# Moving the split of the contexts from GpSimd to VectorE, and loading the query bias in rows, in a cross-attention kernel on one Trainium2 core

## The chip, the cores and the metric

The kernel runs on 1 core of one Trainium2 chip. A time is device microseconds (us) of one execution, and a kernel's time is the median of its runs. The core has five engines that the text names: TensorE (PE in the profile; PEld are its weight loads), VectorE (DVE), ScalarE (ACT), GpSimd (POOL) and SyncE (SP), which issues most of the DMAs. An engine name with a q (SPq, ACTq) is that engine's sequencer issuing a DMA.

## The reference

The inputs are x (16, 100, 128), a context (16, 1444, 128), weights Wq, Wk, Wv (128, 1024), Wo (1024, 128), and biases. For each of 16 batches and 16 heads of 64:

```
q = (pre_q @ Wq + bq).reshape(b, ql, H, D_Q)
k = (pre_k @ Wk + bk).reshape(b, kl, H, D_Q)
v = (pre_k @ Wv + bv).reshape(b, kl, H, D_Q)
scores = jnp.einsum('bqhd,bkhd->bhqk', q, k) / jnp.sqrt(jnp.float32(D_Q))
attn = jax.nn.softmax(scores, axis=-1)
ctx = jnp.einsum('bhqk,bkhd->bqhd', attn, v).reshape(b, ql, H * D_Q)
out = ctx @ Wo + bo
x = pre_q + out
```

A layer norm over the last axis with gamma and beta follows. pre_q is x and pre_k the context.

## The kernel before

**The algebra.** Keys and values are never formed. A prologue multiplies each head's Wq and Wk parts into a 128x128 matrix a_sb, and its Wv and Wo parts into m_sb. A batch's queries are then x times a_sb plus a bias term (gb_sb, made from Wk and bq), its scores are those queries against the context itself, and its output is (attention times context) times m_sb. Operands in 32 bits are split into a high and a low half in 16 bits (c_hi and c_lo of the context, g_hi and g_lo of the queries, p_hi and p_lo of the attention), and three products of halves stand for one.

**Tiles.** The 1600 rows (16 heads by 100 queries) of a batch are cut into tiles of 128 rows. Two batches make 25 tiles, the middle one shared, so there are N = 200 tiles. The loop over n runs on all engines at once, each with its own program. For tile n TensorE makes scores (nine matmuls of 482 columns, line 631); VectorE takes the row maximum (L917); ScalarE takes the exponentials (L1072) with their sum; VectorE inverts the sum (L923, L925); ScalarE writes p_hi (L1080) and the tail of p_lo (L1087); VectorE writes the rest of p_lo (lo_part, L932). SyncE transposes p_hi and p_lo by DMA (pt_hi, L420; pt_lo, L429), in one queue in the order written: pt_lo of tile n-1, then pt_hi of tile n. Four tiles later (LAG) TensorE multiplies them with the context (L670), two tiles at a time, and ScalarE takes the result (L1110).

**What waits for what.** scores(n) writes the half of PSUM that exp(n-2) reads, so it waits for it. exp(n) waits for the row maximum, and for the p_lo of tile n-2, whose buffer it overwrites. VectorE's order in step n is: row_max(n), lo_part(n-1), row_inverse(n), then whatever that step has besides.

**Windows.** The 12 or 13 tiles of a batch are its window w; r is the place of a tile in it. Work for the next batch w+1 is spread over the window: query projections at r = 1 to 4 on TensorE, copied by ScalarE (L1096), split by GpSimd; c_hi of the next context by ScalarE in three groups of four context tiles at r = 4, 6, 7 (L1016); sums of magnitudes of the context after it by ScalarE at r = 5 and 8 (L1023); c_lo by GpSimd in two instructions for each group: c_raw times alpha into c_scaled (L1254), minus c_hi (L1258); then c_tail (L1243, L1245). SyncE transposes c_hi (ct_hi, L400) at r = 7 and c_lo (ct_lo, L411) at r = 8 (9 in the first window). The first context's c_lo is made by VectorE in the prologue, one instruction for each group (L881). TensorE has the output projection of batch w-1 at r = 6 to 9.

**The prologue.** Banks of PSUM are numbered jobs: 0 to 3 transposed weights, J_A and J_B the head products (two banks each), J_X the first x transposed, with the bias product beside it (query_bias, L543), then the query projections J_G (L480). Each is emptied by VectorE or ScalarE. bq goes by two DMAs, element by element, into bq_pairs, whose columns stand for heads (L1000). TensorE's order is J_A, query_bias, spread_context_max, the x transposes, J_B, J_G.

Of the kernel before, what the change touches and what calls it, by code (L numbers as in the profile page):

```python
# [12 lines left out]
P = 128  # L13
# [11 lines left out]
def cross_attention_kernel(nc, x, ctx_in, Wq, bq, Wk, bk, Wv, bv, Wo, bo, gamma, beta, out):  # L25
# [45 lines left out]
    CT_HI_AT = 7  # L71
    CT_LO_AT = 8
# [66 lines left out]
    with ExitStack() as es:  # L139
# [58 lines left out]
        c_scaled = sb("c_scaled", [P, TG * D])  # L198
# [5 lines left out]
        p32 = sb("p32", [P, P32S, SCOREW])  # L204
        bq_pairs = sb("bq_pairs", [P, PAIRS, 2])
# [23 lines left out]
        s_bq = sem("bq_loaded")  # L229
        s_bvl = sem("bv_loaded")  # L230
# [44 lines left out]
        s_cs = sem("context_scaled")  # L275
# [35 lines left out]
        J_A, J_X, J_B = 4, 6, 7  # L311
        J_G = J_B + 2
# [6 lines left out]
        BY_SCALAR = [1, 3, J_A, J_A + 1, J_X, J_B + 1, J_V1, J_M2]  # L319
# [142 lines left out]
        def _(pe):  # L462
# [76 lines left out]
            def query_bias(bank):  # L539

                pe.wait_ge(s_bq, 32)
                for c in range(PAIRS):
                    mm = pe.matmul(bank[:, XG * QL + 2 * c:XG * QL + 2 * c + 2], w_t[1][:, c, :], bq_pairs[:, c, :],  # L543
                                   start=True, stop=True)
                return mm
# [278 lines left out]
        def _(dve):  # L824
# [46 lines left out]

            empty(0)
# [4 lines left out]
            empty(J_B)  # L877
# [56 lines left out]

            def take_rows(b):
# [16 lines left out]
            for n in range(N + 1):  # L952
# [40 lines left out]
        def _(act):  # L993
            for half in range(2):
                cols = slice(half * D_H // 2, (half + 1) * D_H // 2)
                act.dma_start(w_raw[1][:, cols], Wk[:, cols]).then_inc(s_w[1][half], 16)
            act.wait_ge(s_bqz, 1)
            for i in range(2):
                rows = slice(HEAD_DIM * i, HEAD_DIM * i + HEAD_DIM)
                act.dma_start(bq_pairs[rows, :, i:i + 1], bq.rearrange("(c i p o) -> i p c o", i=2, p=HEAD_DIM, o=1)[i],  # L1000
                              allow_slow_non_contiguous=True).then_inc(s_bq, 16)
# [38 lines left out]
            for k in (1, 3, J_A, J_A + 1):  # L1040
                empty(k)
            a_sum(0)
            empty(J_X)
            act.activation(gb_sb[:, :], job_bank(J_X)[:, XG * QL:XG * QL + H], ACT.Copy, scale=SCALE).then_inc(s_gb, 1)
            for g in range(NT):
                context_hi(0, g)
            empty(J_B + 1)
# [127 lines left out]
        def _(pool):  # L1175
# [54 lines left out]
            def leave_m_lo(g):  # L1230
                heads, at = slice(HG * g, HG * g + HG), c_scaled[:, :].rearrange("p (n w) -> p n w", w=P)
# [15 lines left out]
            def context_lo(b):  # L1247
                par = b % 2
                pool.wait_ge(s_al, b + 1)
                for g in range(NT):  # L1250
                    tiles = slice(TG * g, TG * g + TG)
                    if NT * b + g > NT:
                        pool.wait_ge(s_cl, NT * (b - 1) + g)
                    pool.tensor_scalar(c_scaled[:, :], c_raw[:, par, tiles, :].rearrange("p t d -> p (t d)"),  # L1254
                                       alpha[:, par:par + 1], 1.0, ALU.mult, ALU.mult).then_inc(s_cs, 1)
                    pool.wait_ge(s_cs, NT * (b - 1) + g + 1)
                    pool.wait_ge(s_chi, NT * b + g + 1)
                    pool.tensor_tensor(c_lo[:, par, tiles, :].rearrange("p t d -> p (t d)"), c_scaled[:, :],  # L1258
                                       c_hi[:, par, tiles, :].rearrange("p t d -> p (t d)"), ALU.subtract).then_inc(s_cl, 1)
                pool.wait_ge(s_cl, NT * b)  # L1260
                context_tail(b)

# [101 lines left out]
```

## Time and profile before

| | |
|---|---|
| median of 3 runs | 870.35 us (869.59 to 874.36) |
| the profiled execution's own time | 871.59 us |
| its span, first to last instruction | 869.8 us |
| mean granted TensorE clock | 0.998 |

The profile is of one execution. The table of its busy times says how much of the span each engine worked; DMA issues, waits and branches do not count as busy. Idle time of an engine is put down to what ended it.

### The profile page before, as it was taken

The numbers are of one execution on the slowest core, as the hardware profiler recorded it, in microseconds if no ns is written. First come the engines' busy times: TensorE is split into PE (matmuls) and PEld (weight loads), VectorE is DVE, ScalarE is ACT, GpSimd is POOL, SyncE is SP. The second block draws the span as 40 slices with busy tenths as digits, with TensorE's granted clock in tenths as the row PEclk, the third lists the DMA queues.
The fourth block names the chain that finished last, engine by engine and source line by source line (L and its number), as shares of the span: only waits on it lengthen the run. The fifth ranks groups of instructions, "written<-read, shape, count | busy, mean of one in ns | idle before, by whom it ended". The sixth has DMA issues, their size and how long they took to land.

```text
span 869.8 us, 19632 instructions
## 1 busy us (share of the span) xinstructions
PE 846.3 (97%) x7306; PEld 605.2 (70%) x7306; DVE 774.7 (89%) x938; ACT 779.6 (90%) x1132; POOL 569.1 (65%) x575
## 2 busy tenths in 40 slices
PE   7999999999999999999999999999999999999996
PEld 6676776767677766777667776776767777677675
DVE  4988888999989989999899998999899999999984
ACT  5899999989999989999989999998989989999983
POOL 2283997949566693867749586694956669397301
PEclk9999999999999999999999999999999999999999
DMA  7899999999999999999999999999999999999985
GB/s 198 186 211 192 195 210 189 216 200 223 215 209 217 217 204 224 209 226 211 205 213 221 216 208 229 198 227 217 213 215 220 205 233 208 222 188 217 209 183 117
DMA packets 683939, 180.80 MB, mean 208 GB/s; under 512 B 654596, under 2 KB 683076, under 8 KB 683844
## 3 DMA queue, kind: packets, MB, share of 16 engines
q1 hardware_dynamic: 682372, 179.01, 105.7%
q8 instruction: 59, 0.97, 0.5%
q10 hardware_dynamic: 1344, 0.53, 0.3%
q14 instruction: 36, 0.29, 0.1%
q0 software_dynamic: 128, 0.01, 0.0%
HBM read 15.35 MB, written 0.82 MB: 19 GB/s over the span
## 4 chain that ended last, share of the span: by engine, by line
PE 52%; ACT 14%; DVE 13%; DMA 8%; issue 7%; SPq 4%; ACTq 0%; POOLq 0%; POOL 0%; DVEq 0%
PE ps L670 25%; PE ps L631 22%; DMA pt_hi<-p_hi 7%; DVE p_lo L932 6%; ACT p L1072 6%; ACT p_hi L1080 5%; DVE nmax L917 4%; SPq L429 2%; PE ps L495 2%; PE ps L488 2%; SPq L420 1%; ACT unused L1023 1%; DMA bq_pairs<-in_L_xattn_bq_dram 1%; DVE rsum L923 1%; ACT o_t L1110 1%
## 5 line engine op out<-in xcount | busy, mean ns | idle before, releaser
L932 DVE SCALAR_TENSOR_TENSOR p_lo<-p,rinv,p_hi 128x1444 f16<-128x1444 f32 x200 | 370.9, 1855 | 7.5 <-ACT p_hi L1080 7.0
L917 DVE TENSOR_REDUCE nmax<-ps 128x1 f32<-128x1446 f32 x200 | 330.0, 1650 | 18.8 <-PE ps L631 18.3
L1080 ACT ACTIVATE p_hi<-p,rinv 128x1444 f16<-128x1444 f32 x200 | 300.0, 1500 | 32.1 <-DVE rinv L925 28.5
L1072 ACT ACTIVATE p<-ps,nmax 128x1446 f32<-128x1446 f32 x200 | 292.2, 1461 | 17.8 <-DVE nmax L917 15.4
L670 PE MATMUL ps<-pt_hi,c_hi 128*128 128x256 f16 (+1 forms) x1232 | 252.9, 261 | 11.4 <-DMA pt_hi<-p_hi 9.0
L670 PE MATMUL ps<-pt_hi,c_lo 128*128 128x256 f16 (+1 forms) x1232 | 253.0, 261 | 0.0
L631 PE MATMUL ps<-ct_hi,g_hi 128*128 128x482 f16 (+3 forms) x624 | 155.5, 367 | 0.8 <-DVE g_lo L892 0.7
L631 PE MATMUL ps<-ct_lo,g_hi 128*128 128x482 f16 (+3 forms) x624 | 154.9, 366 | 0.0
L631 PE MATMUL ps<-ct_hi,g_lo 128*128 128x482 f16 (+3 forms) x624 | 154.9, 366 | 0.0
L670 PEld LDWEIGHTS ps<-pt_hi,c_hi 128*128 128x128 f16 x1232 | 114.1, 98 | 50.4 <-issue 16.8
L1204 POOL TENSOR_TENSOR g_raw<-g_raw,gb_b 128x400 f32<-128x400 f32 x60 | 81.0, 1350 | 96.2 <-ACT g_raw L1096 96.2
L670 PE MATMUL ps<-pt_lo,c_hi 128*128 128x256 f16 (+1 forms) x1232 | 138.7, 261 | 0.0
L670 PEld LDWEIGHTS ps<-pt_hi,c_lo 128*128 128x128 f16 x1232 | 113.6, 97 | 28.4
L670 PEld LDWEIGHTS ps<-pt_lo,c_hi 128*128 128x128 f16 x1232 | 109.5, 98 | 12.0
L631 PEld LDWEIGHTS ps<-ct_hi,g_lo 128*128 128x128 f16 (+1 forms) x624 | 58.6, 98 | 64.1
L631 PEld LDWEIGHTS ps<-ct_lo,g_hi 128*128 128x128 f16 (+1 forms) x624 | 58.6, 98 | 64.2 <-DMA ct_lo<-c_lo 0.4
L1211 POOL TENSOR_TENSOR g_lo<-g_raw,g_hi 128x400 f16<-128x400 f32 x60 | 88.8, 1480 | 4.8
L1266 POOL TENSOR_SCALAR vpe<-mv 100x1 f32<-100x1 f32 x16 | 3.8, 238 | 122.4 <-DVE mv L950 122.3
L1221 POOL TENSOR_TENSOR xT<-o_t,xT 128x400 f16<-128x400 f32 x52 | 67.6, 1300 | 4.2
L1087 ACT ACTIVATE p_lo<-p,rinv 128x72 f16<-128x72 f32 x200 | 69.8, 349 | 0.0
L631 PEld LDWEIGHTS ps<-ct_hi,g_hi 128*128 128x128 f16 (+1 forms) x624 | 52.3, 99 | 24.9 <-issue 2.0
L1258 POOL TENSOR_TENSOR c_lo<-c_scaled,c_hi 128x512 f16<-128x512 f32 x45 | 65.1, 1447 | 4.3 <-ACT c_hi L1016 0.5
(138 smaller groups left out, 863.0 us busy)
## 6 DMA issues: line engine op xcount, KB each, us to landing
c_raw<-in_ctx_dram SPq DMA_DIRECT2D x32, 256.0 KB, 6.1
pt_hi<-p_hi SPq DMA_TRANSPOSE x200, 3.5
pt_lo<-p_lo SPq DMA_TRANSPOSE x200, 3.7
c_raw<-in_ctx_dram SPq DMA_DIRECT2D x16, 192.0 KB
c_raw<-in_ctx_dram SPq DMA_DIRECT2D x48, 18.0 KB
out_dram<-late_sb SPq DMA_DIRECT2D x16, 50.0 KB
x_sb<-in_x_dram SPq DMA_DIRECT2D x1, 600.0 KB
o_t<-in_L_xattn_Wq_dram SPq DMA_DIRECT2D x2, 256.0 KB, 4.5
```

What stands on the lines that cost most here:

```text
L429: sp.dma_start_transpose(pt_lo[:, u % PTS, place, :, :], p_lo[:, n % LOS, :]).then_inc(s_tl[n % LOS], 16)
L631: mm = pe.matmul(ps[at:at + rows, bank + k, 0:e - a], g, ct, start=(part == 0), stop=(part == 2))
L670: mm = pe.matmul(out_t if rows < P else split(out_t, 2, P), weights, moving, start=(first and i == 0), stop=(last and i == len(products) - 1))
L917: dve.tensor_reduce(nmax[:, n % RING:n % RING + 1], ps[:, bank:bank + 3, 0:KEYW], AX.XY, ALU.max, negate=True).then_inc(s_nm, 1)
L932: dve.scalar_tensor_tensor(out=p_lo[:, n % LOS, 0:KL], in0=p32[:, n % P32S, 0:KL], scalar=rinv[:, i:i + 1], in1=p_hi[:, par, 0:KL], op0=AL ...
L1072: act.activation(p32[:, n % P32S, :].rearrange("p (k w) -> p k w", w=KEYW), ps[:, bank:bank + 3, 0:KEYW], ACT.Exp, bias=nmax[:, i:i + 1], ...
L1080: act.activation(p_hi[:, par, 0:KL], p32[:, n % P32S, 0:KL], ACT.Copy, scale=rinv[:, i:i + 1]).then_inc(s_hi, 1)
L1087: act.activation(p_lo[:, n % LOS, KL:KL + 2 * KTAIL].rearrange("p (i k) -> p i k", i=2), tail, ACT.Copy, scale=rinv[:, i:i + 1]).then_inc( ...
L1204: pool.tensor_tensor(g_raw[:, heads, :], g_raw[:, heads, :], gb_b[:, par, heads].unsqueeze(2).to_broadcast([P, HG, QL]), ALU.add).then_inc ...
L1211: pool.tensor_tensor(g_lo[:, par, cols], query_group(g), g_hi[:, par, cols], ALU.subtract).then_inc(s_gs, 1)
L1221: pool.tensor_tensor(o16[:, 1, cols], o_t[:, b % 2, cols], o16[:, 0, cols], ALU.subtract).then_inc(s_os, 1)
L1258: pool.tensor_tensor(c_lo[:, par, tiles, :].rearrange("p t d -> p (t d)"), c_scaled[:, :], c_hi[:, par, tiles, :].rearrange("p t d -> p (t ...
```

## The change

context_lo moves to VectorE as one instruction for each group, in the form that the prologue already has, at r = 5, 7 and 8, behind row_inverse; GpSimd keeps only the tail, and waits for the three. bq is loaded as 8 rows of 128 by one DMA, first in ScalarE's queue, transposed by TensorE behind the warm-up into JOB_BANK, and copied by VectorE into bq_pairs. In the prologue J_B is done ahead of query_bias, VectorE instead of ScalarE empties J_X and makes gb_sb, and ScalarE instead of VectorE empties the first bank of J_B. c_scaled is renamed left_scaled; other uses of it stay.

```diff
+    CLO_AT = (5, 7, 8)
...
-        J_A, J_X, J_B = 4, 6, 7
-        J_G = J_B + 2
+        J_A, J_B, J_X = 4, 6, 8
+        J_G = J_X + 1
...
-        BY_SCALAR = [1, 3, J_A, J_A + 1, J_X, J_B + 1, J_V1, J_M2]
+        BY_SCALAR = [1, 3, J_A, J_A + 1, J_B, J_B + 1, J_V1, J_M2]
...
+            pe.wait_ge(s_bq, 16)
+            pe.transpose(ps[:, JOB_BANK, 0:PAIRS], bq_rows[:, :], ident[0:PAIRS, 0:PAIRS]).then_inc(s_bqt, 1)
...
             head_products_by_two(w_t[0], w_t[1], 0, J_A)
+            pe.wait_ge(s_bqp, 2)
+            head_products_by_two(w_t[0], w_t[1], 2, J_B)
             query_bias(take(J_X))
             spread_context_max(job_bank(J_G + 2), 0)
             transpose_x(0, J_X).then_inc(s_fill, 1)
-            head_products_by_two(w_t[0], w_t[1], 2, J_B)
...
+            dve.wait_ge(s_bqt, 1)
+            dve.wait_ge(s_bqz, 1)
+            for i in range(2):
+                rows = slice(HEAD_DIM * i, HEAD_DIM * i + HEAD_DIM)
+                dve.tensor_copy(bq_pairs[rows, :, i], ps[rows, JOB_BANK, 0:PAIRS]).then_inc(s_bqp, 1)
             empty(0)
             empty(2)
...
-            empty(J_B)
+            empty(J_X)
+            dve.tensor_scalar(gb_sb[:, :], job_bank(J_X)[:, XG * QL:XG * QL + H], SCALE, None, ALU.mult).then_inc(s_gb, 1)
...
+            def context_lo(b, g):
+                par, tiles = b % 2, slice(TG * g, TG * g + TG)
+                dve.wait_ge(s_chi, NT * b + g + 1)
+                if b > 1:
+                    dve.wait_ge(s_pv, RESULTS * (b - 1))
+                    dve.wait_ge(s_chl, b - 1)
+                dve.scalar_tensor_tensor(out=c_lo[:, par, tiles, :].rearrange("p t d -> p (t d)"),
+                                         in0=c_raw[:, par, tiles, :].rearrange("p t d -> p (t d)"), scalar=alpha[:, par:par + 1],
+                                         in1=c_hi[:, par, tiles, :].rearrange("p t d -> p (t d)"),
+                                         op0=ALU.mult, op1=ALU.subtract).then_inc(s_cl, 1)
...
+                if r in CLO_AT and w + 1 < B:
+                    context_lo(w + 1, CLO_AT.index(r))
...
+            act.dma_start(bq_rows[:, :], bq.rearrange("(c p) -> c p", p=P)).then_inc(s_bq, 16)
...
-            act.wait_ge(s_bqz, 1)
-            for i in range(2):
-                rows = slice(HEAD_DIM * i, HEAD_DIM * i + HEAD_DIM)
-                act.dma_start(bq_pairs[rows, :, i:i + 1], bq.rearrange("(c i p o) -> i p c o", i=2, p=HEAD_DIM, o=1)[i],
-                              allow_slow_non_contiguous=True).then_inc(s_bq, 16)
...
-            for k in (1, 3, J_A, J_A + 1):
+            for k in (1, 3, J_A, J_A + 1, J_B, J_B + 1):
                 empty(k)
             a_sum(0)
-            empty(J_X)
-            act.activation(gb_sb[:, :], job_bank(J_X)[:, XG * QL:XG * QL + H], ACT.Copy, scale=SCALE).then_inc(s_gb, 1)
             for g in range(NT):
                 context_hi(0, g)
-            empty(J_B + 1)
...
-                    pool.tensor_scalar(c_scaled[:, :], c_raw[:, par, tiles, :].rearrange("p t d -> p (t d)"),
-                                       alpha[:, par:par + 1], 1.0, ALU.mult, ALU.mult).then_inc(s_cs, 1)
...
-                    pool.tensor_tensor(c_lo[:, par, tiles, :].rearrange("p t d -> p (t d)"), c_scaled[:, :],
-                                       c_hi[:, par, tiles, :].rearrange("p t d -> p (t d)"), ALU.subtract).then_inc(s_cl, 1)
...
                 if b < B:
-                    context_lo(b)
+                    pool.wait_ge(s_cl, NT * b)
+                    context_tail(b)
```

## Rows read from the trace of the kernel before

**Rows 1.** Page, part 1: busy time, share of the span, instructions

```profile
PE 846.3 (97%) x7306; PEld 605.2 (70%) x7306; DVE 774.7 (89%) x938; ACT 779.6 (90%) x1132; POOL 569.1 (65%) x575
```

**Rows 2.** Busy time by stretch: length, engines, granted clock, DMA share, GB/s

```profile
25.00:50.00 25.00, 23.87 (x164) 16.25 (x164) 23.17 (x30) 22.56 (x32) 7.06 (x7) 1.00 0.94 190
50.00:850.00 800.00, 789.75 (x6897) 561.99 (x6895) 732.14 (x869) 736.99 (x1068) 551.53 (x545) 1.00 1.09 211
```

**Rows 3.** Waits of the whole span: us in total, times, longest

```profile
DVE rsum L923 <- ACT p L1072: 37.2, 85, 1.2
PE ps L670 <- DMA pt_hi<-p_hi: 9.0, 13, 1.8
```

**Rows 4.** Timeline of the prologue, all engines: start, length, instructions merged

```profile
1.69 1.54 ACTq L1000 DMA_DIRECT2D bq_pairs<-in_L_xattn_bq_dram  x2
...
10.55 1.92 PE L543 MATMUL ps<-bq_pairs,early_sb 128*128 128x2 f32 x16 [1.33 <-DMA bq_pairs<-in_L_xattn_bq_dram]
...
12.39 0.87 PE L517 MATMUL ps<-ident,x_sb 100*128 100x100 f32 x4
...
12.96 0.16 DVE L863 RECIPROCAL alpha<-unscale 128x1 f32<-128x1 f32 x1
...
13.77 1.94 ACT L1016 ACTIVATE c_hi<-c_raw,alpha 128x512 f16<-128x512 f32 x3
...
15.73 2.09 SPq L400 DMA_TRANSPOSE ct_hi<-c_hi  x1
15.92 2.07 DVE L881 SCALAR_TENSOR_TENSOR c_lo<-c_raw,alpha,c_hi 128x512 f16<-128x512 f32 x3
...
18.01 1.41 SPq L411 DMA_TRANSPOSE ct_lo<-c_lo  x1
...
19.12 0.57 DVE L892 TENSOR_TENSOR g_lo<-g_raw,g_hi 128x400 f16<-128x400 f32 x1
...
19.95 0.78 PE L631 MATMUL ps<-ct_hi,g_hi 128*128 128x482 f16 x3 [0.69 <-DVE g_lo L892]
...
21.23 0.79 PE L631 MATMUL ps<-ct_lo,g_hi 128*128 128x482 f16 x3
```

**Rows 5.** DMA issues of the first 25 us: count, KB, us to landing

```profile
o_t<-in_L_xattn_Wk_dram ACTq DMA_DIRECT2D x2, 256.0 KB, 4.7
...
bq_pairs<-in_L_xattn_bq_dram ACTq DMA_DIRECT2D x2, 2.0 KB, 7.1
...
ct_hi<-c_hi SPq DMA_TRANSPOSE x1, 3.7
ct_lo<-c_lo SPq DMA_TRANSPOSE x1, 3.2
```

**Rows 6.** Groups by line: busy us, mean ns, then idle before

```profile
L932 DVE SCALAR_TENSOR_TENSOR p_lo<-p,rinv,p_hi 128x1444 f16<-128x1444 f32 x200 | 370.9, 1855 | 7.5 <-ACT p_hi L1080 7.0
...
L881 DVE SCALAR_TENSOR_TENSOR c_lo<-c_raw,alpha,c_hi 128x512 f16<-128x512 f32 x3 | 2.1, 745 | 0.0
...
L801 DVE COPY xT<-ps 128x400 f32<-128x400 f32 x3 | 1.7, 555 | 0.0
...
L1258 POOL TENSOR_TENSOR c_lo<-c_scaled,c_hi 128x512 f16<-128x512 f32 x45 | 65.1, 1447 | 4.3 <-ACT c_hi L1016 0.5
L1254 POOL TENSOR_SCALAR c_scaled<-c_raw,alpha 128x512 f32<-128x512 f32 x45 | 56.8, 1263 | 3.1
```

**Rows 7.** Line 932 alone: ns min/median/max, first and last start

```profile
L932 DVE SCALAR_TENSOR_TENSOR p_lo<-p,rinv,p_hi x200: 1711/1723/2612, 27.8 to 855.6; 128x1444 f16<-128x1444 f32 x100
```

**Rows 8.** Timeline behind row_inverse of tile 120 (r = 8), each engine's own

```profile
531.50 0.16 DVE L925 RECIPROCAL rinv<-rsum 128x1 f32<-128x1 f32 x1
531.74 1.66 DVE L917 TENSOR_REDUCE nmax<-ps 128x1 f32<-128x1446 f32 x1
533.32 1.71 DVE L932 SCALAR_TENSOR_TENSOR p_lo<-p,rinv,p_hi 128x1444 f16<-128x1444 f32 x1
...
533.93 1.45 ACT L1072 ACTIVATE p<-ps,nmax 128x1446 f32<-128x1446 f32 x1
...
537.87 1.49 SPq L429 DMA_TRANSPOSE pt_lo<-p_lo  x1
```

More of the change, by code:

```diff
@@ L197, in cross_attention_kernel @@
         c_top = sb("c_top", [P, 1], BF16)
-        c_scaled = sb("c_scaled", [P, TG * D])
+        left_scaled = sb("left_scaled", [P, TG * D])
         alpha = sb("alpha", [P, 2])
@@ L204, in cross_attention_kernel @@
         p32 = sb("p32", [P, P32S, SCOREW])
+        bq_rows = sb("bq_rows", [PAIRS, P])
         bq_pairs = sb("bq_pairs", [P, PAIRS, 2])
@@ L229, in cross_attention_kernel @@
         s_bq = sem("bq_loaded")
+        s_bqt = sem("bq_turned")
+        s_bqp = sem("bq_pairs_ready")
         s_bvl = sem("bv_loaded")
@@ L274, in cross_attention_kernel @@
         s_chi = sem("context_hi_ready")
-        s_cs = sem("context_scaled")
         s_cl = sem("context_lo_ready")
@@ L539, in query_bias @@
             def query_bias(bank):
-                pe.wait_ge(s_bq, 32)
+                pe.wait_ge(s_bqp, 2)
                 for c in range(PAIRS):
@@ L571, in _ @@
             head_products_by_two(w_t[0], w_t[1], 0, J_A)
+            pe.wait_ge(s_bqp, 2)
+            head_products_by_two(w_t[0], w_t[1], 2, J_B)
             query_bias(take(J_X))
@@ L1230, in leave_m_lo @@
             def leave_m_lo(g):
-                heads, at = slice(HG * g, HG * g + HG), c_scaled[:, :].rearrange("p (n w) -> p n w", w=P)
+                heads, at = slice(HG * g, HG * g + HG), left_scaled[:, :].rearrange("p (n w) -> p n w", w=P)
                 pool.wait_ge(s_mh, g + 1)
@@ L1245, in context_tail @@
                 pool.tensor_copy(c_tail[0:2 * KTAIL, par, :], c_hi[0:2 * KTAIL, par, KT - 1, :]).then_inc(s_chl, 1)
[L1247 to L1253, printed above, removed]
-                    pool.tensor_scalar(c_scaled[:, :], c_raw[:, par, tiles, :].rearrange("p t d -> p (t d)"),
-                                       alpha[:, par:par + 1], 1.0, ALU.mult, ALU.mult).then_inc(s_cs, 1)
-                    pool.wait_ge(s_cs, NT * (b - 1) + g + 1)
-                    pool.wait_ge(s_chi, NT * b + g + 1)
-                    pool.tensor_tensor(c_lo[:, par, tiles, :].rearrange("p t d -> p (t d)"), c_scaled[:, :],
-                                       c_hi[:, par, tiles, :].rearrange("p t d -> p (t d)"), ALU.subtract).then_inc(s_cl, 1)
-                pool.wait_ge(s_cl, NT * b)
-                context_tail(b)
             def inverse_deviation(b):
@@ L1271, in leave_lo @@
                 n, w = raw.shape[1], raw.shape[2]
-                at = c_scaled[:, 0:n * w].rearrange("p (n w) -> p n w", w=w)
+                at = left_scaled[:, 0:n * w].rearrange("p (n w) -> p n w", w=w)
                 if i:
```

## The prediction

> **What bounds the kernel now.** I read the busy times first [rows 1]. Three engines lie near 90% and TensorE stands at 97%, so one must ask which of them the others follow. The stretches answer it [rows 2]: from 50 to 850 us TensorE is busy 789.75 of 800 us, at the full granted clock. No change elsewhere can take more than 800 - 789.75 = 10.3 us out of that stretch. VectorE has 732.1 there, so 68 us of room; ScalarE has 63.
>
> Next come the waits [rows 3]. Of TensorE's idle time 9.0 us in 13 pieces is a wait for pt_hi, the transposed p_hi. These transposes stand in one queue, behind the pt_lo of the tile before, which needs VectorE's p_lo: this is the way by which a late VectorE could reach TensorE. The row above it shows the room: VectorE waited 85 times for ScalarE's exponentials, 37.2 us in all.
>
> Last the prologue's timeline [rows 4], because TensorE's order is serial there and half of the change is in it: the bias product starts at 10.55, after 1.33 us of waiting for bq_pairs.
>
> **The change in the windows: what moves.** It is made 45 times (15 contexts, 3 groups). GpSimd loses 65.1 + 56.8 = 121.9 us of busy time [rows 6] and falls from 569.1 to about 447. No wait of TensorE's on it is in sight, so on the path this is worth 0.
>
> VectorE gets 45 instructions. The same form with the same operands is in the trace, 745 ns [rows 6]: 45 x 0.745 = 33.5 us. Two terms correct this. First, p_lo takes 1.723 us at the median and 1.855 in the mean [rows 6, 7]; the excess is 370.9 - 200 x 1.723 = 26.3 us. In the timeline a long p_lo begins while a GpSimd instruction is under way and ends about 1.72 us after that one's end. Of the 26.3 us, 7.9 (17 of the 200 instructions of rows 7) fall on starts within one of the two removed instructions, and go. Second, the new instruction has the same kind of operands and may find GpSimd at work. At the 45 places behind row_inverse I read what GpSimd still had to run of other work: at r = 5 mostly 0.0 to 0.45 us, once 0.9, in sum 4.3 us; at r = 7 and 8 almost only the removed instructions. So VectorE gets 33.5 - 7.9 + 4.3 = 29.9 us, and goes from 774.7 to about 804.6, 92.5%.
>
> The Trainium skill, page SBUF — State Buffer, section "SBUF: two separate sides", says that VectorE and GpSimd share a port pair under an exclusive lock, which a VectorE instruction with two SBUF inputs takes for its whole length against a GpSimd one that reads SBUF. The trace agrees, with p_lo between 1711 and 2612 ns [rows 7]. By that rule VectorE's addition is the 29.9 us above; without it, it would be the plain 33.5 us. The rule speaks against the change in one point, that the new instructions too shut GpSimd out, 33.5 us in all.
>
> **What of the 29.9 us lies on the path.** I take r = 8, with tile 120 [rows 8]. row_inverse is over at 531.66. Before, the next row maximum starts at 531.74 and is over at 533.40, but the exponentials start only at 533.93: ScalarE is held by p_hi and its own extra at this r, the magnitude sum. With 0.745 - 0.10 = 0.65 us ahead of it (consecutive instructions overlap by some 0.1 us in the timeline) the maximum starts at about 532.2, is over at about 533.85, and the exponentials still start at 533.93. At r = 7 c_hi of the step before takes the place of the sum; the same reckoning gives at most 0.05 us. At r = 5 the sum is there again. So the next scores see nothing.
>
> What is late next is p_lo, by 0.45 us here: from 533.32 to 533.8, over by 535.5. SyncE issues its transpose at 537.87 [rows 8], 2.4 us later, because it works off ct_hi, ct_lo and the context loads. Behind it is pt_hi, equally untouched. At r = 5 and 7 I find in the timeline the same order, SyncE 0.5 to 3 us behind p_lo, except in the last but one window, which has no loads. The step after has the wait for the exponentials (0.3 us, part of the 37.2 [rows 3]) and no extra, which gives the lag back.
>
> The other users of c_lo: ct_lo at r = 8 stands behind pt_hi, which needs p_hi, which ends 1.5 us after row_inverse, and the new instruction ends after 0.65. The tail waits on GpSimd until r = 8; behind it stands the layer norm of r = 10. Neither is late. If this cover were gone, all 29.9 us would count. I take 0, nearest to rows 8, and keep for the range -9.0 (no pt_hi wait is left [rows 3]) and +11 (below).
>
> In the first window VectorE also empties a bank behind each of tiles 8 to 10, and TensorE waits for the last of them. The c_lo of tile 8 costs this chain about 0.3 us; a p_lo of 2.51 us in it, hit by the removed GpSimd work, gives 0.3 back. Sum 0.
>
> **The prologue, step by step.** (1) One DMA stands ahead of the Wk halves, so they land up to some 0.45 us later; they were there before TensorE came to them. bq_rows itself is not in the trace. Its bounds: landed before the warm-up ends at 4.35, cost 0, or as late as a 256 KB half, 0.75 + 4.7 = 5.45 [rows 5], which would hold TensorE for about 0.5 us. It moves 4 KB, so I take 0. [...]
>
> (2) J_B follows J_A at once, at about 9.2, and fills the wait up to 10.55; query_bias runs from about 10.4 to 12.3 instead of to 12.47 [rows 4]. alpha is hardly earlier, 13.1 as before: the 1.3 us won on bq are spent on J_B, which has only changed its place.
>
> (3) ScalarE no longer empties J_X and makes gb_sb between alpha and c_hi. c_hi starts at about 13.15 instead of 13.77 and ends at about 15.1 instead of 15.71: 0.6 us.
>
> (4) ct_hi goes out at 15.1 instead of 15.73 and lands 3.7 later [rows 4, 5], at 18.8 instead of 19.4.
>
> (5) VectorE empties J_X (0.56 us [rows 6]) and makes gb_sb by about 14.05, then c_lo in 2.07 us: over at 16.1 instead of 17.99. g_lo is over at about 17.9 instead of 19.69, 1.8 us. The projections, no longer behind J_B, start at about 14 instead of 15.2, and keep ahead.
>
> (6) So the first scores wait for ct_hi and not for g_lo: 18.9 instead of 19.95. Their last part waits for ct_lo. Its issue stands behind that of ct_hi, which takes 2.09 us: 15.1 + 2.1 = 17.2 instead of 18.01, landed 3.2 later at 20.4, where before the part started at 21.23. Gain 0.8 us.
>
> What follows, VectorE's and ScalarE's chain over the first tiles, starts from these scores, so the 0.8 us are kept. Bounds: 0, if the loads ahead hold the transposes, and 1.8, the whole of VectorE's lead.
>
> **Sum.** The profiled execution took 871.59 us (span 869.8), 1.24 above the median of the runs. 871.59 - 0.8 (prologue) + 0 (windows) = 870.8; against the median, 870.35 - 0.8 = 869.5 us. A change of 0.5% is 4.35 us, about what a measurement of this kernel can tell, with three runs that spread from 869.59 to 874.36.
>
> **The rivals.**
> *The transposes become late (slower).* Place: SyncE's queue at r = 5 to 10. If SyncE is less far behind than I read, a p_lo that is 0.65 to 0.75 us late delays pt_lo, the pt_hi behind it, and then TensorE. Once for each of 15 windows: 15 x 0.75 = 11 us, 869.5 + 11 = 880.5. It decides from the point where SyncE's lag behind p_lo is under 0.5 us. For it: TensorE waits for pt_hi already, 13 times, and ScalarE and VectorE are close together. Against: those waits come from tiles at r = 4 and 10, where the lag is 1 to 4 us. Chance 0.08.
>
> *VectorE becomes the bound (slower).* With 29.9 us on the path, 899. Against it: 68 us of room, and a mean load of 92.5% under TensorE's 97%. Chance 0.02.
>
> *The freed GpSimd and the shorter p_lo take the pt_hi waits away (faster).* 869.5 - 9.0 = 860.5. Against: those waits stem from context loads and transposes in SyncE's queue, which stay. Chance 0.05; another 0.03 for a part of it together with the full 1.8 us of the prologue, some 865.
>
> *The prologue gives nothing,* because the DMA queues hold ct_lo: 870.35. Inside the band. Chance 0.17. The forecast as worked out has 0.65.
>
> Faster by over 0.5%: 0.05 + 0.03 = 0.08. Slower: 0.08 + 0.02 = 0.10. Within: 0.65 + 0.17 = 0.82.
>
> **Range.** The forecast and the flat prologue lie from 868.5 (gain 1.8) to 870.4. With a few pt_hi waits more or fewer, some 2.5 us to either side, I take 866.8 to 873.0. Outside lie the rivals, 0.18.
>
> **What the profile will show.** Right: L1258 and L1254 gone for c_lo, 45 new VectorE instructions near 0.75 to 0.85 us in the mean, p_lo's mean down from 1855 to about 1815 ns, VectorE near 805 us, GpSimd near 450, TensorE still over 789 of the middle 800 us. The first scores start near 18.9 and their last part near 20.4; no wait for bq. Wrong: more than 13 waits for pt_hi or more than 12 us of them, scores waiting for exponentials, SyncE waiting for p_lo at r = 5, 7 or 8, or TensorE held at its first weight transpose by bq_rows.

## The result, and the profile after

The changed kernel takes 876.15 us (median of 19 runs, 871.26 to 880.92), the kernel before in the same series 871.07 us (median of 19, 869.04 to 877.61). The ratio is 1.0048, with a 95% interval of 1.0031 to 1.0065. The forecast was 869.5 us, in a range of 866.8 to 873.0: the change costs 0.5%, where a small gain within the noise was expected.

The profiled execution of the changed kernel took 880.92 us (span 879.1), the longest of its 19 runs, 4.8 us above their median. Differences between its trace and that of before are therefore likely too large, and what follows takes other traces beside it. First its busy times, the middle stretch, and the two waits that the prediction rested on:

```profile
PE 851.6 (97%) x7307; PEld 608.4 (69%) x7307; DVE 798.2 (91%) x986; ACT 781.3 (89%) x1131; POOL 441.1 (50%) x485
```

```profile
50.00:850.00 800.00, 785.07 (x6843) 557.33 (x6843) 748.60 (x903) 732.98 (x1059) 422.49 (x452) 1.00 1.09 209
```

```profile
DVE rsum L935 <- ACT p L1090: 26.1, 62, 1.0
...
PE ps L676 <- DMA pt_hi<-p_hi: 13.5, 19, 2.0
```

VectorE has 23.5 us more and GpSimd 128 us less than in [rows 1]. In the middle 800 us VectorE still has 51 us of room, yet TensorE is idle for 14.9 us instead of 10.3 [rows 2]. Its waits for pt_hi grew from 13 to 19, and from 9.0 to 13.5 us. VectorE's own wait for the exponentials shrank from 37.2 to 26.1 us [rows 3]: part of the new work went into it. The rest had to go elsewhere.

The groups of the two kinds of instruction (busy, mean ns, then idle before):

```profile
L944 DVE SCALAR_TENSOR_TENSOR p_lo<-p,rinv,p_hi 128x1444 f16<-128x1444 f32 x200 | 364.5, 1822 | 6.5 <-ACT p_hi L1098 6.1
...
L953 DVE SCALAR_TENSOR_TENSOR c_lo<-c_raw,alpha,c_hi 128x512 f16<-128x512 f32 x45 | 36.8, 818 | 0.0
```

The prologue's timeline (start, length), which answers to [rows 4]:

```profile
0.73 0.60 ACTq L1019 DMA_DIRECT2D bq_rows<-in_L_xattn_bq_dram  x1
...
4.29 0.27 PE L570 MATMUL ps<-ident,bq_rows 8*128 8x8 f32 x1
...
8.48 0.66 PE L513 MATMUL ps<-ident,o_t 128*128 128x128 f32 x4 [1.11 <-DMA o_t<-in_L_xattn_Wk_dram]
...
13.16 2.27 PE L546 MATMUL ps<-bq_pairs,early_sb 128*128 128x2 f32 x16
...
16.06 1.95 ACT L1037 ACTIVATE c_hi<-c_raw,alpha 128x512 f16<-128x512 f32 x3 [0.75 <-DVE alpha L869]
...
16.76 5.41 PE L483 MATMUL ps<-xT,a_sb 128*128 128x100 f32 x32 [0.91 <-DVE xT L797]
...
22.01 0.78 PE L637 MATMUL ps<-ct_hi,g_hi 128*128 128x482 f16 x3
```

bq itself is there in time, 4.29, but the second half of Wk is not: TensorE waits 1.11 us for it at 8.48. The bias product starts at 13.16 instead of 10.55, c_hi at 16.06 instead of 13.77, the first scores at 22.01 instead of 19.95. The projections take 5.41 us (4.05 before) at a lower granted clock, 0.73 against 0.93 from 15 to 20 us. Not all of this is the change: among the traces whose prologue is that of before, the first scores start between 18.52 (e8) and 23.58 (f2).

### The profile page after: what moved, and what is told of

Its sections match the earlier page's. It is cut to its first block, busy times and chain, and to the rows that moved or that the text cites. A ratio compares the mean times of both kernels' runs of the same rounds, so it can differ in the third digit from the quotient of the medians.

```text
span 879.1 us, 19574 instructions
## 1 busy us (share of the span) xinstructions
PE 851.6 (97%) x7307; PEld 608.4 (69%) x7307; DVE 798.2 (91%) x986; ACT 781.3 (89%) x1131; POOL 441.1 (50%) x485
## 4 chain that ended last, share of the span: by engine, by line
PE 43%; DVE 18%; ACT 15%; DMA 9%; issue 8%; SPq 6%; ACTq 0%; POOLq 0%; POOL 0%; DVEq 0%
PE ps L676 20%; PE ps L637 17%; DVE p_lo L944 9%; DMA pt_hi<-p_hi 8%; DVE nmax L929 6%; ACT p L1090 6%; ACT p_hi L1098 5%; SPq L432 3%; PE ps L498 2%; SPq L423 2%; PE ps L491 1%; DVE rsum L935 1%; ACT c_hi L1037 1%; DVE rinv L937 1%; SPq L403 1%
## 5 line engine op out<-in xcount | busy, mean ns | idle before, releaser
L944 DVE SCALAR_TENSOR_TENSOR p_lo<-p,rinv,p_hi 128x1444 f16<-128x1444 f32 x200 | 364.5, 1822 | 6.5 <-ACT p_hi L1098 6.1
L1098 ACT ACTIVATE p_hi<-p,rinv 128x1444 f16<-128x1444 f32 x200 | 299.9, 1500 | 33.3 <-DVE rinv L937 29.9
L676 PE MATMUL ps<-pt_hi,c_hi 128*128 128x256 f16 (+1 forms) x1232 | 254.1, 261 | 15.7 <-DMA pt_hi<-p_hi 13.5
L1229 POOL TENSOR_TENSOR g_lo<-g_raw,g_hi 128x400 f16<-128x400 f32 x60 | 83.0, 1384 | 4.8
L1239 POOL TENSOR_TENSOR xT<-o_t,xT 128x400 f16<-128x400 f32 x52 | 71.5, 1376 | 4.2
L1261 POOL COPY c_tail<-c_lo 128x128 f16<-128x128 f16 x16 | 4.7, 291 | 117.3 <-DVE c_lo L953 101.4
```

What stands on the lines that cost most here:

```text
L676: mm = pe.matmul(out_t if rows < P else split(out_t, 2, P), weights, moving, start=(first and i == 0), stop=(last and i == len(products) - 1))
L944: dve.scalar_tensor_tensor(out=p_lo[:, n % LOS, 0:KL], in0=p32[:, n % P32S, 0:KL], scalar=rinv[:, i:i + 1], in1=p_hi[:, par, 0:KL], op0=AL ...
L1098: act.activation(p_hi[:, par, 0:KL], p32[:, n % P32S, 0:KL], ACT.Copy, scale=rinv[:, i:i + 1]).then_inc(s_hi, 1)
L1229: pool.tensor_tensor(g_lo[:, par, cols], query_group(g), g_hi[:, par, cols], ALU.subtract).then_inc(s_gs, 1)
L1239: pool.tensor_tensor(o16[:, 1, cols], o_t[:, b % 2, cols], o16[:, 0, cols], ALU.subtract).then_inc(s_os, 1)
```

## The experiments

Eighteen runs were made, each against the kernel before on the same chip, most with 12 executions (e6 has 4; e7, e12 and g1 have 6). Labels are shortened to their first part. "VectorE" and "GpSimd" say who makes the c_lo of the windows. The last two columns are from the one profiled execution of each: first scores to the scores of tile 199, and TensorE's waits for pt_hi over the whole span. The scores' time differs by 0.8 us between two executions of one kernel (e4, e11), and goes from 825.5 to 827.5 us over the five traces whose windows are those of before (before, e1, e4, e5, e11).

| run | c_lo | ratio to before [95%] | scores 0 to 199, us | pt_hi waits, us, times |
|---|---|---|---|---|
| before | GpSimd | | 827.5 | 9.0, 13 |
| after | VectorE | 1.0048 [1.0031, 1.0065] | 834.8 | 13.5, 19 |
| e1 | GpSimd | 1.0001 [0.9982, 1.0019] | 827.4 | 9.5, 12 |
| e2 | VectorE | 1.0043 [1.0024, 1.0061] | 830.2 | 11.3, 14 |
| e3 | VectorE | 1.0031 [1.0009, 1.0053] | 828.8 | 9.0, 15 |
| e4 | GpSimd | 0.9972 [0.9954, 0.9989] | 826.3 | 8.2, 12 |
| e5 | GpSimd | 1.0020 [1.0004, 1.0037] | 826.4 | 8.3, 12 |
| e6 | VectorE, twice | 1.0347 [1.0320, 1.0375] | 855.0 | 10.7, 13 |
| e7 | VectorE, GpSimd too | 1.0087 [1.0064, 1.0111] | 832.7 | 10.2, 15 |
| e8 | VectorE in even windows | 1.0036 [1.0016, 1.0056] | 831.4 | 11.8, 17 |
| e9 | VectorE in odd windows | 1.0010 [0.9992, 1.0028] | 827.8 | 9.0, 14 |
| e10 | as e9 | 0.9983 [0.9962, 1.0004] | 830.3 | 11.7, 18 |
| e11 | GpSimd (e4 again) | 0.9983 [0.9960, 1.0005] | 825.5 | 7.7, 10 |
| e12 | VectorE | 1.0085 [1.0056, 1.0113] | 834.7 | 12.5, 18 |
| f1 | GpSimd | 0.9966 [0.9945, 0.9986] | 822.4 | 4.9, 7 |
| f2 | VectorE | 1.0010 [0.9989, 1.0032] | 829.3 | 10.2, 14 |
| f3 | VectorE | 1.0052 [1.0030, 1.0074] | 831.2 | 4.1, 5 |
| f4 | GpSimd | 1.0016 [0.9994, 1.0038] | 830.4 | 6.4, 10 |
| g1 | GpSimd | 0.9932 [0.9915, 0.9949] | 823.2 | 5.1, 10 |
| g2 | VectorE | 0.9996 [0.9981, 1.0012] | 824.9 | 6.2, 11 |

**The two halves of the change.** e1 is the changed kernel with c_lo back on GpSimd; e2 is the kernel before with context_lo, and its call in the loop, on VectorE, and nothing of the new prologue. In e1:

```diff
-                if r in CLO_AT and w + 1 < B:
-                    context_lo(w + 1, CLO_AT.index(r))
...
-                    pool.wait_ge(s_cl, NT * b)
-                    context_tail(b)
+                    context_lo(b)
```

> The new prologue with c_lo left on GpSimd. My theory now (two causes): the prologue alone costs the 2.0 us by which the first scores were later (22.0 against 19.95), so the first scores start near 22.0, the middle 800 us keep TensorE busy for about 789.7 us, and the time is about 2 us over that of before (0.25%). The rival, that all the loss is in the windows, expects no difference in time. The rival that all of it is the prologue expects the full 4 to 5 us.

> The old prologue with c_lo on VectorE in the windows. My theory: first scores at 19.95 as before; VectorE lags behind TensorE by 1 to 2 us from r = 6 to r = 0 of the windows of even number, TensorE idle in the middle 800 us about 13 to 15 us instead of 10.3; time about 2 to 3 us over before. The rival that the windows are hidden as I had forecast expects the time of before within 1 us and 10 us of idle time.

e1 is 1.0001, e2 1.0043, and their intervals do not meet. The windows carry the loss, about 3.7 us; the new prologue as written is worth nothing that an interval of 0.2% to either side would show. The 2 us that e1 expected did not come: its first scores start at 19.75.

**The order of the first loads.** e3 is the changed kernel with the load of bq_rows behind the Wk halves, its turn on TensorE behind the weight transposes, and VectorE's copies behind its two weight copies; e4 (and e11, the same kernel again) has that prologue and leaves c_lo on GpSimd. e5 is the kernel before with one load ahead whose data nothing uses (GpSimd only waits for it to land):

```diff
-            act.dma_start(bq_rows[:, :], ...).then_inc(s_bq, 16)
             for half in range(2):
                 ... Wk halves
+            act.dma_start(bq_rows[:, :], ...).then_inc(s_bq, 16)
```

> The changed kernel with the load of bq_rows moved behind the two halves of Wk in ScalarE's queue, and its transpose and copies behind the weight transposes. If the load ahead made the second half of Wk late, the weight transposes end near 7.1 us as before instead of 9.1, the first scores start 2 to 3 us earlier than in the changed kernel, near 19 to 20, and the time is 2 us under the changed kernel. Rival: Wk came late by chance in that one execution, or by the order of the head products; then the first scores stay near 22.

> The new prologue with bq_rows behind Wk, and c_lo left on GpSimd. My theory: this takes away both losses and keeps the prologue's gain: first scores near 19.0 to 19.5, middle as before, time 0.5 to 1 us under before. If the new order of the prologue has a loss of its own beside the load, it is at or above before.

> The kernel before with one DMA more, the load of bq in rows ahead of the Wk halves on ScalarE's queue; its data is used by nothing, everything else stays. Theory (a small load ahead makes the Wk halves land late enough to hold TensorE in the weight transposes or in the first head products): TensorE waits 0.5 to 1.2 us for a Wk half, and the median is above before by up to 1 us, ratio 1.000 to 1.0012, which five rounds may not tell from nothing. Rival (the prediction's: the halves are there in time): no wait for Wk in the profile, ratio 1.000.

> The new prologue with bq_rows behind Wk, and c_lo of the windows left on GpSimd, a second time on another day's chip. The first time it was 0.9972 of before, interval 0.9954 to 0.9989. If the gain is the prologue's: 0.996 to 0.9985 again. If it was chance: within 0.1% of 1.

e5 costs 0.20%, 1.7 us, for a load of 4 KB. TensorE's timeline in e5:

```profile
5.60 1.45 PE L512 MATMUL ps<-ident,o_t 128*128 128x128 f32 x8 [0.39 <-DMA o_t<-in_L_xattn_Wk_dram]
7.86 0.66 PE L512 MATMUL ps<-ident,o_t 128*128 128x128 f32 x4 [0.81 <-DMA o_t<-in_L_xattn_Wk_dram]
```

It waits 1.20 us for Wk, where the kernel before has no such wait (it waits 0.57 us for Wq at 4.92), and the next wait, for early_sb, is over at 9.29 instead of 8.06. e1, with the same load ahead, waits 1.22 us for Wk; no trace without this load waits for Wk. With the load behind Wk the same prologue gains 0.28%, and 0.17% the second time (this interval just reaches 1). So the new prologue is two opposite things of some 1.5 to 2.5 us each, by the middle values.

**Dose.** e6 makes each of the 45 instructions twice, once into a spare buffer. e7 leaves GpSimd's two instructions running as well, into a spare buffer.

```diff
+                dve.scalar_tensor_tensor(out=c_spare[:, :], in0=..., scalar=..., in1=...).then_inc(s_cp, 1)
                 dve.scalar_tensor_tensor(out=c_lo[:, par, tiles, :]..., in0=..., scalar=..., in1=...).then_inc(s_cl, 1)
```

```diff
-                    context_tail(b)
+                    context_lo_again(b)
...
+                    pool.tensor_scalar(c_scaled[:, :], c_raw..., alpha..., 1.0, ALU.mult, ALU.mult)
+                    pool.tensor_tensor(c_spare[:, :], c_scaled[:, :], c_hi..., ALU.subtract)
```

> The kernel before with c_lo of the windows on VectorE, and each of the 45 instructions made twice, first into a spare buffer that nothing reads. Theory (VectorE's own time in the even windows is what costs, carried over to the first tile of the next window, where p_hi and its transpose come late): with one set of 45 the ratio to before was 1.0043, some 3.7 us. The lag has no slack left to be absorbed by, so a second set costs more than the first: its 45 x 0.7 = 31 us of VectorE time add 5 us or more, time 880 to 890, and the waits for pt_hi grow to over 20. Rival (only the place matters: the row maximum behind the instruction, one wait each, or GpSimd's later tail): the second set changes little, time 875 to 877, ratio under 1.006.

> The kernel before with c_lo of the windows on VectorE, while GpSimd still runs its two instructions for each group, the second into a spare buffer that nothing reads. It tells what GpSimd's relief gave. Theory: little. VectorE's p_lo keeps the 7.9 us that its overlaps with GpSimd cost, and some new instructions stretch too, so VectorE lies about 8 to 15 us above the 798 us that it had without GpSimd's share, and the time goes to 876 to 880. Rival (the loss comes from something that became late on GpSimd, the tail of c_lo, or from a changed order of its other work): with GpSimd's old load the tail is still later, and the time rises by much more, over 882, with TensorE waiting for the tail. Rival (GpSimd's relief already gave something of weight): over 880 by waits for pt_hi alone.

Busy times of e2, e7 and e6, in this order:

```profile
PE 848.8 (97%) x7306; PEld 607.8 (70%) x7306; DVE 798.0 (91%) x983; ACT 780.7 (89%) x1132; POOL 440.8 (51%) x485
```

```profile
PE 850.2 (97%) x7306; PEld 605.8 (69%) x7306; DVE 812.3 (93%) x983; ACT 780.3 (89%) x1132; POOL 571.4 (65%) x575
```

```profile
PE 857.9 (96%) x7306; PEld 605.2 (67%) x7306; DVE 832.8 (93%) x1028; ACT 780.5 (87%) x1132; POOL 447.7 (50%) x485
```

The price rises with the load. The first 23.3 us on VectorE (774.7 to 798.0) cost 3.7 us, 0.16 us for each. The next 34.8 (to 832.8) cost 0.0304 x 871 = 26.5 us, 0.76 for each; they stand in the same steps as the first, so more load and more delay in one place are not told apart. e7's 14.3 us above e2 cost 3.8 us, 0.27 for each. In e6 the exponentials themselves are late (waits):

```profile
ACT p L1097 <- DVE nmax L920: 59.7, 75, 2.5
...
PE ps L673 <- ACT o_t L1135: 7.6, 12, 1.1
```

Both theories missed the size of e6, and there are 13 waits for pt_hi and not over 20. Some 4 us of e6 are one place in the first window: TensorE waits 2.62 us, until 63.98, for the bank that VectorE empties (L804), and its clock falls behind that wait. e7 shows that GpSimd's relief was worth 0.44% by the middle values, as much as what is left to pay: without it the move would have cost twice as much. The groups of c_lo on VectorE, in e2 and in e7:

```profile
L942 DVE SCALAR_TENSOR_TENSOR c_lo<-c_raw,alpha,c_hi 128x512 f16<-128x512 f32 x45 | 38.2, 849 | 0.3 <-issue 0.3
```

```profile
L944 DVE SCALAR_TENSOR_TENSOR c_lo<-c_raw,alpha,c_hi 128x512 f16<-128x512 f32 x45 | 45.7, 1015 | 0.3 <-issue 0.3
```

The same instruction takes 1015 ns in the mean with GpSimd's two at work and 849 without, and 750 at r = 7 and 8 of e2, where GpSimd mostly rests. The Trainium skill, page SBUF — State Buffer, section "SBUF: two separate sides", has a VectorE instruction with two SBUF inputs and a GpSimd one that reads SBUF exclude each other on the ports they share; this pair agrees with it.

**Which windows.** e8 does c_lo on VectorE when w is even (24 instructions), e9 when w is odd (21); e10 is e9 with the prologue of e4.

```diff
-                if r in CLO_AT and w + 1 < B:
+                if r in CLO_AT and w + 1 < B and w % 2 == 0:
```

> The kernel before with c_lo on VectorE only in the even windows (24 instructions, 8 contexts), on GpSimd in the odd ones. Theory (the lag of the even windows is what costs, since there it is carried into the next window; in the odd windows it is given back): nearly all of the 3.7 us, 874.5 to 876, ratio 1.003 to 1.0045. Rival (each instruction costs the same wherever it stands): half of it and a little, 24/45 x 3.7 = 2.0 us, ratio 1.0023.

> The kernel before with c_lo on VectorE only in the odd windows (21 instructions, 7 contexts), on GpSimd in the even ones. Theory (the lag of the odd windows is given back before it meets a late transpose): within 0.1% of before, 871 to 873. Rival (each instruction costs the same): 21/45 x 3.7 = 1.7 us, ratio 1.002. Third possibility: below before, since p_lo is less stretched by GpSimd's two instructions in these windows, ratio 0.999.

> The changed kernel with bq_rows loaded behind Wk and its transpose behind the weight transposes, and c_lo on VectorE in the odd windows alone, on GpSimd in the even ones. It is a candidate for the fastest. Theory (ledger of steps: in the odd windows TensorE's step at r = 7 is 5.3 us long and takes the lag back, in the even ones every step from r = 9 on is shorter than VectorE's work): ratio to before 0.997 to 0.999, the gain of the prologue less about 0.1%. Rival (every one of the instructions costs alike, and the same prologue with all of them on VectorE gave 1.0031): 0.9972 + 21/45 x 0.0059 = 1.000.

Even 1.0036, odd 1.0010. The two intervals overlap, and the rival's values (1.0023 and 1.0020, each instruction at the same price) lie inside them: the times alone do not show that the even windows carry the cost. But e10 against e11, the same prologue with and without the odd windows' instructions, is 0.9983 against 0.9983, so by the middle values the odd windows cost 0.1% or nothing. The traces say more. I add up two lengths for each step, mean over windows 3 to 14: from one tile's first scores to the next one's in the kernel before, and VectorE's work between the row maxima (the sum of its instructions' durations), before and in e2.

| r | even: step | work before | in e2 | odd: step | work before | in e2 |
|---|---|---|---|---|---|---|
| 5 | 3.58 | 4.02 | 5.24 | 3.80 | 3.86 | 4.95 |
| 6 | 4.34 | 3.98 | 3.84 | 4.12 | 4.16 | 4.14 |
| 7 | 4.12 | 4.02 | 4.42 | 5.25 | 4.12 | 4.42 |
| 8 | 4.39 | 3.96 | 4.43 | 4.12 | 3.78 | 4.43 |
| 9 | 4.12 | 3.82 | 3.81 | 4.34 | 3.84 | 3.83 |
| 10 | 3.92 | 4.43 | 4.43 | 3.70 | 4.44 | 4.44 |
| 11 | 3.73 | 4.04 | 4.04 | 3.86 | 4.11 | 4.11 |

In an even window the steps from r = 5 to 9 last 20.55 us. VectorE had 19.80 us of work in them and has 21.74 in e2: 0.75 us of slack became 1.19 us of debt, just ahead of r = 10 and 11, which are 0.8 us short in any case. In an odd window r = 7 is long, the sum is 21.63 against 21.77, and the debt is 0.14. Both debts come out too large, since consecutive instructions overlap by some 0.1 us and a sum of durations counts that time twice. Counted once, the work of an even window goes from 19.55 to 21.07 us, 1.0 us of slack to 0.5 us of debt, and that of an odd one from 19.48 to 21.07, which leaves 0.6 us of slack. The sign is the same: the even windows cannot give the lag back before r = 10, the odd ones can. The lag itself (row maximum's start less the scores' end, same windows) says the same: at r = 9 of even windows 0.06 us before and 1.52 in e2, at r = 10 0.33 and 1.12; at r = 9 of odd windows 0.22 and 0.81, at r = 10 0.15 and 0.14, given back. Into r = 0 of the window behind an even one it carries 1.69 us instead of 1.05.

VectorE's timeline in the changed kernel, tiles 80 to 84 (window 6, r = 5 to 9):

```profile
371.75 1.05 DVE L953 SCALAR_TENSOR_TENSOR c_lo<-c_raw,alpha,c_hi 128x512 f16<-128x512 f32 x1
372.73 1.65 DVE L929 TENSOR_REDUCE nmax<-ps 128x1 f32<-128x1446 f32 x1
374.30 1.89 DVE L944 SCALAR_TENSOR_TENSOR p_lo<-p,rinv,p_hi 128x1444 f16<-128x1444 f32 x1
...
380.64 0.75 DVE L953 SCALAR_TENSOR_TENSOR c_lo<-c_raw,alpha,c_hi 128x512 f16<-128x512 f32 x1
381.31 1.66 DVE L929 TENSOR_REDUCE nmax<-ps 128x1 f32<-128x1446 f32 x1
382.88 1.71 DVE L944 SCALAR_TENSOR_TENSOR p_lo<-p,rinv,p_hi 128x1444 f16<-128x1444 f32 x1
384.59 0.15 DVE L935 TENSOR_SCALAR rsum<-psums 128x1 f32<-128x1 f32 x1
384.78 0.16 DVE L937 RECIPROCAL rinv<-rsum 128x1 f32<-128x1 f32 x1
384.89 0.75 DVE L953 SCALAR_TENSOR_TENSOR c_lo<-c_raw,alpha,c_hi 128x512 f16<-128x512 f32 x1
385.56 1.66 DVE L929 TENSOR_REDUCE nmax<-ps 128x1 f32<-128x1446 f32 x1
```

From 380.64 on no row has idle time before it. The scores of the tile at 385.56 ended at 384.17: the step is 4.25 us of work without a gap, and nothing is given back. The first instruction, at r = 5, takes 1.05 us: it meets GpSimd at work, as the prediction reckoned (mean of the 15 at this place 0.95 us, of the other 30 0.75).

**The place within the step.** e12 has the instruction ahead of row_inverse, where VectorE often waits for the exponentials.

```diff
+                if r in CLO_AT and w + 1 < B:
+                    context_lo(w + 1, CLO_AT.index(r))
                 row_inverse(n)
```

> The kernel before with c_lo of the windows on VectorE at the same r, but ahead of row_inverse instead of behind it, where VectorE often waits for the exponentials. Theory (VectorE's time in steps that are shorter than its work is what costs, wherever in the step it stands): about as with the instruction behind row_inverse, 1.003 to 1.006; p_hi of the same tile is later, so more waits for pt_hi. Rival (the place behind row_inverse costs, because the row maximum stands behind it; here the instruction fills VectorE's own wait): ratio 1.000 to 1.002.

1.0085, twice the loss of e2. The row maximum is not all that must be protected: at r = 8 and 9 of even windows it starts 0.35 and 0.39 us earlier than in e2 (at r = 7 and 10 it starts 0.45 and 0.23 us later), while p_hi stands behind the new instruction, and ScalarE's wait for the inverse grows from 29.4 us in e2 to 42.1. That fits p_hi as the carrier; it does not show it.

**Through which queue.** f1 and f2 leave all but one context tile of the transpose of c_lo out, from the third context on; f3 and f4 issue ct_lo at r = 9; g1 and g2 load only one context tile of each group of four, from the fourth context on.

```diff
+                if b > 1:
+                    sp.dma_start_transpose(ct_lo[:, par, 0:P]..., c_lo[:, par, 0, :]).then_inc(s_ctl[par], 16)
+                    return
...
-    CT_LO_AT = 8
+    CT_LO_AT = 9
...
+                if b > 2:
+                    e = a + 1
```

> The kernel before, but from the third context on the transpose of c_lo moves one context tile of twelve; the other eleven keep what stood there, so that part of the computation is left out. It is the ground for the next run: SyncE's queue has a transpose of about 1.5 us less in each of 14 windows. Theory (queue): the waits for pt_hi shrink from 8 to 5 us or less and the ratio is 0.996 to 0.999. Rival (the queue is not what makes pt_hi late): the waits stay near 8 us, ratio 1.000.

> The same cut of ct_lo as in the run before it, and c_lo of the windows on VectorE; the same part of the computation is left out. What counts is its ratio over that of the run before it, which with the full transpose was 1.0043. Theory (VectorE's lag reaches TensorE through SyncE's full queue): the two come within 0.15% of each other, of which 0.06% is the first window, where nothing was cut. Rival (the lag reaches TensorE in another way): the full 0.4% between the two stays.

> The kernel before with c_lo of the windows on VectorE, and ct_lo issued at r = 9 in every window instead of r = 8, behind the pt_hi of r = 9. Theory (queue): that pt_hi is 1.5 us earlier, which is more than VectorE's lag; the loss of 1.0043 falls to 1.001 to 1.003, unless the pt_hi of r = 10 is then late for the next one. Rival (not the queue): 1.0043 as before, between 1.003 and 1.006.

> The kernel before with ct_lo at r = 9 in every window, c_lo on GpSimd. It says what the place of ct_lo is worth by itself. Theory: between 0.998 and 1.001, since with c_lo on GpSimd the waits for pt_hi are 8 us in all and only some are at r = 0. If the run before it gains and this one does not, the place of ct_lo matters just where VectorE lags.

> The kernel before, but the loads of the contexts from the fourth on bring one context tile of each group of four; the rest keeps the values of an older context, so that part of the data is left out. It is the ground for the next run. Theory: the pt_hi waits shrink from 8 to 5 us or less, above all those at r = 7 and 8, ratio 0.994 to 0.998. Rival (the loads hold nobody): 1.000.

> The same cut of the loads, and c_lo of the windows on VectorE. What counts is its ratio over that of the run before it, which with the full loads was 1.0043. Theory (the lag of the even windows meets the transposes behind the context loads of the next window): the two come within 0.2% of each other, the first window's 0.06% included. Rival (wherever SyncE's transposes have no slack, a late p_hi or p_lo costs, and no single load or transpose is the place): 0.3 to 0.45% stay.

The pairs differ by 1.0010 / 0.9966 = 1.0044, 1.0052 / 1.0016 = 1.0036 and 0.9996 / 0.9932 = 1.0064, where the full pair has 1.0043. Each quotient is uncertain by 0.2 to 0.3%, from its two intervals. The pair of the loads (g) lies clearly above the 0.2% that its theory left; the pair f2 and f1 lies above its 0.15% by just its uncertainty; f3 itself, with an interval from 1.0030, stands above the 1.001 to 1.003 that was expected of it. So the theories of a single place fall, that of the loads most clearly. A shorter queue makes both kernels faster, by up to 0.7%, and in none of the pairs does the distance between them go away. In f3 the wait only changes its name: 5.9 us for ct_lo at r = 0, beside 4.1 for pt_hi.

What the traces do show is that more of the way to the end leads through VectorE. The chain of work that ended last, by engine, in before and in e2:

```profile
PE 52%; ACT 14%; DVE 13%; DMA 8%; issue 7%; SPq 4%; ACTq 0%; POOLq 0%; POOL 0%; DVEq 0%
PE 46%; DVE 17%; ACT 13%; DMA 9%; issue 8%; SPq 7%; ACTq 0%; POOLq 0%; POOL 0%; DVEq 0%
```

VectorE has 9 to 13% of it in the eight traces with the windows' c_lo on GpSimd, 17 to 19% in the seven with all of it on VectorE and GpSimd relieved, 28% in e7 and 39% in e6. Even windows alone give 18% (e8); odd ones 11% in e9, but 19% in e10.

## Why the prediction was wrong

**The step that failed** is the one under "What of the 29.9 us lies on the path": "I take 0", from the reckoning that the step after has the wait for the exponentials, which "gives the lag back". It was read from tile 120, r = 8 of window 9, an odd window. There it holds: the odd windows alone cost 0.10% (e9). In the even windows the steps from r = 5 to 9 are together shorter than VectorE's work, so that most of the lag stays (1.12 us at r = 10 instead of 0.33, 1.69 instead of 1.05 at the next r = 0), and they alone cost 0.36% (e8); that the cost divides in this way rests on the lags and on the middle values. The value in the place of the 0 is 3.7 us (e2), for 23.3 us more of VectorE's busy time.

- *What moves* was right in its parts: 45 x 0.818 = 36.8 us of new instructions (33.5 + 4.3 = 37.8 predicted), p_lo 6.4 us shorter (7.9). The durations of all its instructions rose by 30.5 in sum (803.7 to 834.2), as forecast, but the busy time only by 23.5 and not 29.9, since it counts overlapping instructions once.
- *At r = 5* I took the addition to be 0.65 us. VectorE's work in this step of the even windows grew by 1.2 us, against a step of 3.6. The 4.3 us that I had for GpSimd's work at this place (0.3 us each) went into the load and not into this reckoning; in e2 the 15 instructions take 1.05 us in the mean.
- *GpSimd's relief, "on the path this is worth 0"*: with GpSimd's two instructions kept (e7) the time is 0.44% longer, 3.8 us, by way of VectorE's instructions, which are 14.3 us longer in busy time. The 3.7 us of the windows are what is left after this credit.
- *The first window, "Sum 0"*: 0.5 us in each of after, e2 and e3, none in e9, which leaves this window alone. TensorE waits 0.77 us for the bank that VectorE empties behind its new instruction (L520 at 63.38).
- *The rival "the transposes become late"* had the right sign, and its mark is there (19 waits for pt_hi, 13.5 us, over both bounds that the prediction set as signs of an error; e3, with 9.0 us in 15, shows it hardly), but too low a chance, 0.08, and not the right place: it was to decide where SyncE is less than 0.5 us behind p_lo, once for each window, and the pairs f and g show no such single place. *"VectorE becomes the bound"*, given 0.02, is what e6 comes near to at 833 us, with 0.76 us of time for each us; the kernel stood nearer to it than its 68 us of room over a mean suggested.
- *Prologue, step (1)*, cost 0 (bound 0.5): wrong. The halves land late enough to hold TensorE 1.1 to 1.2 us (after, e1, e5), 1.7 us of time in e5. That "they were there before TensorE came to them" was true and said nothing of by how much.
- *Steps (2) to (6)*, gain 0.8 us: too small. Once the load is behind Wk, they give 0.17 to 0.28%, 1.5 to 2.4 us (e11, e4). Step (6) also named the wrong limit. In most traces TensorE goes from the projections straight into the scores (no idle time before 22.01 above); where they are fast, the scores wait for VectorE (e11, 1.29 us for the memset at L908, behind the last g_raw of L875), and start at 18.23.

Between 869.5 and 876.15 lie 6.6 us: 0.8 of the prologue's gain that did not come (gain and load cancel), 3.7 of the windows, 0.7 by which the longer series of before lay above the three runs, and 1.4 that the two halves measured apart don't give: 0.9 of them because the medians lie 5.1 us apart where the ratio of 1.0048 gives 4.2, and the rest is within the 1.5 us of the ratio's interval.

**What stays open.** From tile 0 to tile 199 TensorE is idle for 15.7, 13.5 and 11.2 us in after, e2 and e3, and 10.4 in the mean of before, e1, e4, e5 and e11, most of the difference in waits for pt_hi. Idle time is not all: in e3 it is 0.8 us more, where the scores from tile 0 to 199 take 2.2 us longer than in the mean of those five. The steps that grew most in after, e2 and e3 are r = 7 of the odd windows (1.5 us in sum in the mean), where TensorE waits for tiles made while the lag of the even window still lasts; they grew by 1.6 in e8 and by 0.1 in the mean of e9 and e10. That these waits are the way is read, not shown: cutting what stands in SyncE's queue did not close the distance. Which wait falls where changes from one execution to the next.

The fastest kernel here is e4 (c_lo on GpSimd, bq in rows, loaded behind Wk): 0.9972 and 0.9983 of before in its two series.

## What to carry to other kernels

When work moves to an engine that is 89% busy, add it up step by step against the length of each step of the bounding engine, over a whole period of the schedule (here 25 tiles, not one): a lag is given back only in steps that are longer than the engine's work, and a single step that does so proves nothing for its neighbours. A mean share under the leader's is no room; double the dose in an experiment, and the slope tells how near the edge is. A small load ahead of a large one that TensorE waits for is not free even when the large one used to be early.

## What the runs showed of the hardware

The granted clock can fall after a single wait of 2.0 us in the middle of the kernel, which then costs nearly twice its length. Windows of the changed kernel around its longest wait for pt_hi, over at 241.98 (columns as in [rows 2]):

```profile
240.00:242.00 2.00, 0.02 (x1) 0.05 (x2) 1.97 (x4) 1.12 (x4) 1.74 (x1) 1.00 0.95 213
242.00:244.00 2.00, 2.00 (x13) 1.48 (x14) 1.30 (x2) 2.00 (x2) 0.00 (x0) 0.64 1.22 275
244.00:246.00 2.00, 2.00 (x9) 1.16 (x8) 1.41 (x3) 1.64 (x4) 0.00 (x0) 0.51 1.04 235
246.00:248.00 2.00, 2.00 (x14) 1.17 (x13) 0.35 (x1) 0.98 (x1) 0.00 (x0) 1.00 1.17 242
```

TensorE does nothing for 2 us, and for the next 4 us it has 0.64 and 0.51 of its clock: about (0.36 + 0.49) x 2 = 1.7 us lost on top. In the kernel before, the wait at this place was 1.22 us and no such fall followed.

It does not follow every such wait. e6 has two waits of 2.6 us. Behind the one that is over at 63.98 the clock falls in the same way; behind the one that is over at 541.03 it stays:

```profile
64.00:66.00 2.00, 2.00 (x9) 1.09 (x10) 2.00 (x2) 1.30 (x4) 0.15 (x1) 0.63 1.08 246
...
542.00:544.00 2.00, 2.00 (x26) 1.67 (x25) 1.81 (x2) 2.00 (x3) 0.00 (x0) 1.00 1.13 257
```

These two falls are the only ones in the 20 traces between 25 us and the last scores; none of the waits of 1.0 to 1.9 us was followed by one.

In the prologue the granted clock also decides what a faster start is worth. The 32 projections took 3.79 us from 13.16 in e11 and 6.67 us from 13.41 in e4, the same kernel; the granted clock from 15 to 20 us was 1.00 and 0.56. In the timelines of e2, e3, e4, e6 and e7 they end between 20.1 and 20.6 us, whether they start at 13.4 or at 15.0: there, what was won on the start was given back to the clock. e8 and f4 start at 13.8 and end at 18.6 and 18.8, so it is not given back in every execution.
